# Attention scores of a two-layer kernel on two 64-row halves of TensorE

## The chip, the core and the metric

The kernel runs on one core of one Trainium2 chip. A core has five engines that run side by side and wait for each other by semaphores: TensorE (PE in the rows; its weight loads are PEld), VectorE (DVE), ScalarE (ACT), GpSimd (POOL) and SyncE (SP), which here only starts DMAs. The metric is the device time in microseconds, before as the median of three runs; lower is better.

## The reference, cut to what matters

There are 4096 tokens of 256 values (16 batches of 256). Each layer adds attention over a context and then a feed-forward part; only attention is touched here.

```
def _L0_xattn_ref(query, key, value, mask, Wq, bq, Wk, bk, Wv, bv, Wo, bo):
    ...
    q = proj_split(query, Wq, bq)
    k = proj_split(key, Wk, bk)
    v = proj_split(value, Wv, bv)
    scores = jnp.einsum('bhqd,bhkd->bhqk', q, k) * scale
    scores = jnp.where(mask == 0, jnp.float32(-1000000000.0), scores)
    probs = jax.nn.softmax(scores, axis=-1)
    attn = jnp.einsum('bhqk,bhkd->bhqd', probs, v)
    ...
x = x + _L0_xattn_ref(_layernorm(x, axis=-1), ctx_1024, ctx_1024, mask_1x1xSxS2_if1, ...)
x = x + _L0_ffn_ref(_layernorm(x, axis=-1), ...)
x = x + _L1_xattn_ref(_layernorm(x, axis=-1), ctx_1024, ctx_1024, ...)
x = x + _L1_ffn_ref(_layernorm(x, axis=-1), ...)
```

There are 16 heads of 16 values. In layer 0 the 256 queries of a batch attend to its 256 keys. In layer 1 attention runs over the 16 batches at one position, so the 256 tokens of a unit are 16 positions by 16 batches, and only the 16 by 16 blocks on the diagonal count. Layer 0's feed-forward part routes each token to 4 of 16 experts.

## The kernel before, in words

One program runs four stages, one after another: `attention` for layer 0 (`l0`), `routed_experts`, `attention` for layer 1 (`l1`) and `gated_ffn`. The change lies in `attention` alone, which both layers call.

`attention` works through 16 units of 256 tokens in a software pipeline. An iteration `u` has 16 steps `k`, one for each head, and in it work for several units stands side by side: at step `k`, TensorE makes the transposed scores of head `k` of unit `u` (L841, keys on the output's partitions) and the plain scores of head `k` of unit `u+2` (L874, queries on the output's partitions). Both are two matmuls, one for each half of 128 rows of output. The plain scores serve for the row maximum alone (VectorE, L715). The maxima are transposed on TensorE (L892, step 1 of the next iteration), split in two float16 parts (L553 on ScalarE, L744 on VectorE) and stacked by DMA under the queries (L385), so that the transposed scores come out with the maximum already taken off. ScalarE takes their exponential (L493) into `pt`, and TensorE multiplies it with the values, four heads at a time (L809 in layer 0, L806 in layer 1). These value products have 32 output columns each and stand side by side on four column groups of the array (`tile_position=(0, 32 * j)`).

Every iteration also holds, between the steps: transposing the normalized x of unit `u+3` (L883, step 0), projecting it to queries (L791 called at steps 4 and 5, called wq below), projecting the context to keys (steps 8 and 9, wk) and to values (steps 12 and 13, wv), the output projection of unit `u-1` (steps 9 and 10, wo), two rounds of transposing outputs (L818, steps 3 and 14), and transposing them again (L911, step 6). Layer 0 has three more pieces for its router: ranks (L852, step 4), a transposition (L830, step 6) and logits (L861, step 12).

Queries and keys are kept as two float16 parts, high and low. The projections leave them in `nat`, ScalarE making the high part (L527) and VectorE the low part (L614). DMAs on SP's queue stack the parts of a head on partitions: `qs` holds them as high, low, high (L392, three DMAs of 32 partitions), `ks` as high, high, low (L398, six DMAs of 16 partitions). One matmul over 96 partitions then gives the three products of the parts. `qs` has two heads on 32 partitions, an even one and an odd one, and `ks` has a place of its own for each of the 16 heads, where the rows of the other head of the pair are zero. Behind the 96 rows come constant rows (`key_rows`, in layer 1 also `query_rows`, which take care of the diagonal blocks) and the rows of the maxima: a plain score uses 96 partitions in layer 0 and 104 in layer 1, a transposed one 100 and 108. Before the pipeline starts, a setup block zeroes `ks` (half on GpSimd, L253, half on VectorE, L268) and loads the constant rows; VectorE waits for them at L276.

`ps_t` and `ps_s` have two buffers each, so a transposed score waits until the exponential two heads back is done (`exp_done`), and a plain score for the maximum two heads back (`max_done`). At step 0 the plain score also waits for the stacked queries and keys (`qs_stacked`, `ks_stacked`), and the transposed one for the stacked maxima (`m_stacked`). Every engine works in the order in which its code is written.

## Time and profile before

| what | value |
|---|---|
| time before, median of 3 runs (lowest to highest) | 1584.51 us (1583.52 to 1587.66) |
| the profiled execution's own time | 1574.22 us |
| its span, first to last instruction | 1572.3 us |
| mean granted TensorE clock in the span | 0.916 of full |
| TensorE matmuls busy | 1146.1 us (73%) |
| TensorE weight loads busy | 863.9 us (55%) |
| VectorE busy | 934.9 us (59%) |
| GpSimd busy | 814.4 us (52%) |
| ScalarE busy | 742.8 us (47%) |
| transposed scores of layer 0, first to last | 85.0 to 464.8 us |
| transposed scores of layer 1, first to last | 1091.1 to 1376.7 us |

The profile shows one execution, which was 10 us shorter than the median. Busy times are sums over the four stages, and the attention of layer 0 and of layer 1 takes some 430 us and 390 us of the span, setup and start included. A matmul's busy time holds its way through the array, so the distance between two starts tells more than its length: matmuls of 256 float16 columns start 0.11 us apart and last 0.27 us.

### The profile page before, as it was taken

What the parts mean: (1) busy time and instruction counts of PE and PEld (TensorE: products, weight loads), DVE (VectorE), ACT (ScalarE), POOL (GpSimd) and SP (SyncE); (2) the same over time, 40 slices, a digit from 0 to 9 for tenths busy, and PEclk for the clock granted to TensorE, in tenths of its full rate; (3) what the DMA queues carried; (4) which work ended last, traced back from release to release, by engine and by line L of the source; (5) the groups of instructions that cost most, each with busy time, mean ns of one, the idle gap of its engine ahead of it and who ended that gap; (6) DMA issues with size and microseconds to landing.
All of it is one profiled execution on the core that took longest, in us unless ns stands there. A gap on an engine that the chain in (4) does not pass through costs nothing. (4 is left out here: it accounts for less than half of the span.)

```text
span 1572.3 us, 35113 instructions
## 1 busy us (share of the span) xinstructions
PE 1146.1 (73%) x11011; PEld 863.9 (55%) x11012; DVE 934.9 (59%) x2206; ACT 742.8 (47%) x1455; POOL 814.4 (52%) x984
## 2 busy tenths in 40 slices
PE   0678788888872276799999998026777777718997
PEld 0355566656541165688887886014566666514555
DVE  4677678778641275566666664137777776435663
ACT  2356566666570154455555554012555555534442
POOL 5222455566466365567776774377666561003442
PEclk9999899999995598999999999567999999969999
DMA  5433323232210447233333343434454442131321
GB/s 156 109 108 77 80 59 86 78 67 69 37 41 21 71 129 140 78 98 106 107 107 104 107 107 89 95 113 132 136 144 140 129 137 64 33 101 54 101 86 55
DMA packets 146544, 147.39 MB, mean 94 GB/s; under 512 B 47912, under 2 KB 122200, under 8 KB 146392
## 3 DMA queue, kind: packets, MB, share of 16 engines
q1 hardware_dynamic: 119792, 95.31, 21.6%
q0 software_dynamic: 17920, 37.84, 9.7%
q10 hardware_dynamic: 8704, 12.58, 2.7%
q8 instruction: 73, 1.20, 0.4%
q14 instruction: 55, 0.45, 0.1%
HBM read 81.69 MB, written 38.27 MB: 76 GB/s over the span
## 5 line engine op out<-in xcount | busy, mean ns | idle before, releaser
L493 ACT ACTIVATE l_pt<-l_ps_t 128x512 f32<-128x512 f32 (+1 forms) x512 | 243.9, 495 | 247.6 <-PE l_ps_t L841 242.1
L715 DVE TENSOR_REDUCE l_mx<-l_ps_s 128x2 f32<-128x512 f32 (+1 forms) x512 | 274.3, 546 | 138.6 <-PE l_ps_s L874 132.7
L1298 PE MATMUL cp_ps_g<-cp_xt,ro_wexp 128*128 128x256 f16 x1920 | 226.7, 275 | 24.4 <-ACT cp_xt L1244 10.3
L1164 POOL DMA_INDIRECT cp_rows<-moe_rows,cp_now x160 | 172.8, 1080 | 95.5 <-POOL cp_now L1159 64.5
L1298 PEld LDWEIGHTS cp_ps_g<-cp_xt,ro_wexp 128*128 x1920 | 183.1, 99 | 55.9 <-issue 32.1
L1216 DVE TENSOR_SCALAR cp_gate<-cp_ps_g,ex_g_bias 128x256 f32<-128x256 f32 x160 | 70.0, 479 | 153.9 <-PE cp_ps_g L1298 153.9
L461 POOL DMA_INDIRECT l_picked<-expert_rows,l_slots x128 | 130.0, 1016 | 56.5 <-issue 36.4
L428 POOL DMA_INDIRECT row_tokens<-l_token_id,ro_pos x128 | 125.9, 984 | 49.2 <-issue 36.7
L1169 POOL TENSOR_TENSOR cp_a_lo<-cp_act_f,cp_a_hi 128x512 f16<-128x512 f32 x80 | 95.5, 1194 | 60.9 <-ACT cp_a_hi L1253 60.1
L874 PE MATMUL l_ps_s<-ro_wexp 96*128 96x256 f16 x512 | 101.6, 282 | 30.6 <-issue 14.6
L1313 PE MATMUL cp_ps_y<-ro_wexp,cp_a_hi 128*128 x640 | 114.9, 274 | 0.0
L1253 ACT CAST cp_a_hi<-cp_act_f 128x512 f16<-128x512 f32 x80 | 49.4, 618 | 128.9 <-DVE cp_act_f L1225 128.9
L841 PE MATMUL l_ps_t<-ro_wexp 100*128 100x256 f16 x512 | 100.7, 280 | 4.7 <-issue 3.3
L1487 POOL TENSOR_TENSOR ff_hlo<-ff_hf,ff_hhi 128x512 f16<-128x512 f32 x48 | 55.9, 1171 | 82.3 <-ACT ff_hhi L1516 82.3
L475 POOL TENSOR_TENSOR l_xin<-l_xin,l_bo 128x512 f32<-128x512 f32 x32 | 40.6, 1268 | 110.0 <-ACT l_xn L571 110.0
L1244 ACT COPY cp_xt<-cp_ps_x 128x1024 f16<-128x1024 f16 x80 | 80.2, 1004 | 34.5 <-PE cp_ps_x L1283 33.8
L874 PE MATMUL l_ps_s<-l_ks,l_qs 104*128 104x128 f16 x512 | 71.5, 229 | 33.4 <-issue 19.9
L1313 PE MATMUL cp_ps_y<-ro_wexp,cp_a_lo 128*128 x320 | 87.2, 273 | 0.0
L1249 ACT ACTIVATE cp_sg<-cp_gate 128x512 f32<-128x512 f32 x80 | 50.4, 630 | 73.9 <-DVE cp_gate L1216 73.9
L1283 PE MATMUL cp_ps_x<-ex_ident,cp_rows 128*128 128x128 f16 x640 | 50.0, 223 | 43.2 <-DMA cp_rows<-moe_rows,cp_now 43.0
L791 PE MATMUL l_ps_b<-l_chi,l_wk 128*128 128x256 f16 x256 | 55.3, 284 | 24.2 <-DVE l_nat L614 23.2
L874 PEld LDWEIGHTS l_ps_s<-ro_wexp 96*128 96x128 f16 x512 | 46.8, 100 | 46.7 <-issue 22.4
(246 smaller groups left out, 2845.0 us busy)
## 6 DMA issues: line engine op xcount, KB each, us to landing
expert_rows<-cp_yout SPq DMA_DIRECT2D x80, 256.0 KB
l_cin<-in_ctxT SPq DMA_DIRECT2D x32, 256.0 KB
ro_raw<-in_gate_up ACTq DMA_DIRECT2D x16, 512.0 KB, 4.0
x<-l_yout SPq DMA_DIRECT2D x64, 128.0 KB
ro_wexp<-l_nat SPq DMA_DIRECT2D x48, 128.0 KB
ro_wexp<-l_nat SPq DMA_DIRECT2D x96, 64.0 KB
l_qs<-l_nat SPq DMA_DIRECT2D x48, 128.0 KB
l_ks<-l_nat SPq DMA_DIRECT2D x96, 64.0 KB
```

The source lines that it names most:

```text
L428: nc.gpsimd.indirect_dma_start(route.table, bass.IndirectOffsetOnAxis(ap=route.pos[:, t, k:k + 1], axis=0), token_id[:, t:t + 1], None).th ...
L461: nc.gpsimd.indirect_dma_start(picked[:, n % 2, q, k], None, y_rows, bass.IndirectOffsetOnAxis(ap=slots[:, n * QT + q, k:k + 1], axis=0)). ...
L493: nc.scalar.activation(pt[:, h % 8], ps_t[:, at % 2, :, 0:span], ACT.Exp).then_inc(exp_done, 1)
L715: nc.vector.reduce_max(mx[:, n % 2, :, 8 * (k % 2) + k // 2], ps_s[:, at % 2, :, 0:span], AX_X).then_inc(max_done, 1)
L841: last = nc.tensor.matmul(ps_t[:, at % 2, kt, 0:span], ks[0:rows_t, u % KQ, key_head, kt * P:kt * P + P], qs[0:rows_t, u % KQ, h // 2, see ...
L874: last = nc.tensor.matmul(ps_s[:, at % 2, q, 0:span], qs[0:rows_s, n % KQ, h // 2, q * P:q * P + P], ks[0:rows_s, n % KQ, key_head, seen], ...
L1164: nc.gpsimd.indirect_dma_start(rows[:, n, h], None, route.rows_dram[:, :], bass.IndirectOffsetOnAxis(ap=now[:, n, h:h + 1], axis=0)).then_ ...
L1169: nc.gpsimd.tensor_tensor(a_lo[:, b], act_f[:, b], a_hi[:, b], ALU.subtract).then_inc(alo_done, 1)
L1216: nc.vector.tensor_scalar(gate[:, b, m], ps_g[:, b, m], g_bias[:, bass.ds(e, 1), m], LIMIT * WS, ALU.add, ALU.min).then_inc(gate_done, 1)
L1244: nc.scalar.copy(xt[:, 1 - b], ps_x[:, 1 - b]).then_inc(xt_copied, 1)
L1298: last = nc.tensor.matmul(ps_g[:, b, m], route.wexp[:, bass.ds(e, 1), cols:cols + P].rearrange("p o n -> p (o n)"), xt[:, b, part, c], sta ...
L1313: last = nc.tensor.matmul(ps_y[:, b, h], a[:, b, c, h * P:h * P + P], route.wexp[:, bass.ds(e, 1), cols:cols + D].rearrange("p o n -> p (o ...
```

## The change

The two heads of a pair get partitions of their own: the even head of each pair lies on partitions 0 to 63 and the odd one on 64 to 127, in `qs` and in `ks`. Each half holds 48 rows of parts, in layer 1 then 8 constant rows, and then the rows of the maxima, one of each part. `ks` needs 8 places in place of 16, and nothing has to be zero, so the zeroing (L253 and L268) and its semaphore go.

A score matmul now covers 64 rows of the array (`tile_position=(0, 0)` or `(64, 0)`). At step `k` the transposed scores are those of head `k` and the plain scores those of head `k ^ 1`, which lies on the other half. Their four matmuls stand in turns: transposed, plain, transposed, plain. All waits of both now stand ahead of the first of them. In layer 0 the ranks (step 4) and logits (step 12), which stood between a step's transposed and plain scores, now stand ahead of both.

The DMAs follow: six of 16 partitions for the queries in place of three of 32, four for the maxima in place of two, and the constant rows go to both halves (two DMAs in layer 0 in place of one, four in layer 1 in place of two), in rows of half the length.

```diff
-        rows_s = 96 + (8 if kinds else 0)
-        rows_t = rows_s + 4
+        data = 3 * DH
+        rows_s = data + (8 if kinds else 0)
+        rows_t = rows_s + 2
...
-                sp.wait_ge(ks_set, 2)
-                sp.dma_start(ks[96:rows_t].rearrange("p b h t -> p (b h t)"), key_rows).then_inc(rows_loaded, 16)
-                if kinds:
-                    sp.dma_start(qs[96:rows_s].rearrange("p b h t -> p (b h t)"), query_rows).then_inc(rows_loaded, 16)
+                for base in (0, 64):
+                    sp.dma_start(ks[base + data:base + rows_t].rearrange("p b h t -> p (b h t)"), key_rows).then_inc(rows_loaded, 16)
+                    if kinds:
+                        sp.dma_start(qs[base + data:base + rows_s].rearrange("p b h t -> p (b h t)"), query_rows).then_inc(rows_loaded, 16)
...
-                nc.gpsimd.memset(ks[:, 2:4], 0.0).then_inc(ks_set, 1)
...
-                nc.vector.memset(ks[:, 0:2], 0.0).then_inc(ks_set, 1)
...
-                            row = rows_s + 2 * i
-                            sp.dma_start(qs[row:row + 2, n % KQ], mt[:, i, :]).then_inc(m_stacked, 16)
+                            for par in range(2):
+                                row = 64 * par + rows_s + i
+                                sp.dma_start(qs[row:row + 1, n % KQ], mt[8 * par:8 * par + 8, i, :]).then_inc(m_stacked, 16)
...
-                            sp.dma_start(qs[32 * i:32 * i + 32, n % KQ].rearrange("d (j m) t -> d j (m t)", m=2),
-                                         nat[:, i % 2].rearrange("p m t -> p (m t)")).then_inc(qs_stacked, 16)
+                            for par in range(2):
+                                row = 64 * par + DH * i
+                                sp.dma_start(qs[row:row + DH, n % KQ].rearrange("d (j m) t -> d j (m t)", m=2),
+                                             nat[64 * par:64 * par + 64, i % 2].rearrange("p m t -> p (m t)")).then_inc(qs_stacked, 16)
...
                         n = u + 2
+                        if live(u):
+                            to = t_at[u, h]
+                            if h == 0:
+                                pe.wait_ge(m_stacked, 64 * (u + 1))
+                            pe.wait_ge(exp_done, c1 + to - 1)
                         if live(n):
-                            at = s_at[n, h]
+                            so = s_at[n, h ^ 1]
                             if h == 0:
-                                pe.wait_ge(qs_stacked, 48 * (n + 1))
+                                pe.wait_ge(qs_stacked, 96 * (n + 1))
                                 pe.wait_ge(ks_stacked, 96 * (n + 1))
-                            pe.wait_ge(max_done, c1 + at - 1)
...
+                            pe.wait_ge(max_done, c1 + so - 1)
...
+                        for half in range(QT):
+                            part = slice(half * P, half * P + P)
+                            seen = part if kinds else slice(0, UNIT)
+                            if live(u):
+                                base = 64 * (h % 2)
+                                last = nc.tensor.matmul(ps_t[:, to % 2, half, 0:span], ks[base:base + rows_t, u % KQ, h // 2, part],
+                                                        qs[base:base + rows_t, u % KQ, h // 2, seen], start=not masks, stop=True, tile_position=(base, 0))
+                                if half:
+                                    last.then_inc(st_done, 1)
+                            if live(n):
+                                base = 64 * (1 - h % 2)
+                                last = nc.tensor.matmul(ps_s[:, so % 2, half, 0:span], qs[base:base + rows_s, n % KQ, h // 2, part],
+                                                        ks[base:base + rows_s, n % KQ, h // 2, seen], start=not masks, stop=True, tile_position=(base, 0))
+                                if half:
+                                    last.then_inc(s_done, 1)
```

Three places show the new order. After the change the transposed scores are L876, the plain ones L882, the projections L793, the transposition of x L892 and the logits L850. The first is TensorE in layer 0, steps 11 and 12 of an iteration in the middle: the scores of step 11 and of step 12 (`ro_wexp` is the memory in which layer 0 keeps `qs` and `ks`), the logits (`l_rw`), and ahead and behind the end of wo and the start of wv. Before:

```order
L791 MATMUL l_ps_a<-l_wo,l_alo 128x256
L841 MATMUL l_ps_t<-ro_wexp 128x256 [waits at_exp_done]
L841 MATMUL l_ps_t<-ro_wexp 128x256
L874 MATMUL l_ps_s<-ro_wexp 128x256 [waits at_max_done]
L874 MATMUL l_ps_s<-ro_wexp 128x256
L841 MATMUL l_ps_t<-ro_wexp 128x256 [waits at_exp_done]
L841 MATMUL l_ps_t<-ro_wexp 128x256
L861 MATMUL l_ps_s<-l_rw,l_xt 128x16 [waits at_exp_done,at_max_done]
L861 MATMUL l_ps_s<-l_rw,l_xt 128x16 x3
L874 MATMUL l_ps_s<-ro_wexp 128x256 [waits at_max_done]
L874 MATMUL l_ps_s<-ro_wexp 128x256
L791 MATMUL l_ps_b<-l_wv,l_chi 128x256 [waits at_kl_done]
```

After:

```order
L793 MATMUL l_ps_a<-l_wo,l_alo 128x256
L876 MATMUL l_ps_t<-ro_wexp 128x256 [waits at_max_done,at_exp_done]
L882 MATMUL l_ps_s<-ro_wexp 128x256
L876 MATMUL l_ps_t<-ro_wexp 128x256
L882 MATMUL l_ps_s<-ro_wexp 128x256
L850 MATMUL l_ps_s<-l_rw,l_xt 128x16 [waits at_exp_done,at_max_done]
L850 MATMUL l_ps_s<-l_rw,l_xt 128x16 x3
L876 MATMUL l_ps_t<-ro_wexp 128x256 [waits at_max_done,at_exp_done]
L882 MATMUL l_ps_s<-ro_wexp 128x256
L876 MATMUL l_ps_t<-ro_wexp 128x256
L882 MATMUL l_ps_s<-ro_wexp 128x256
L793 MATMUL l_ps_b<-l_wv,l_chi 128x256 [waits at_kl_done]
```

The four score matmuls of a step now stand in turns behind one set of waits, and the logits, which parted step 12's four, stand ahead of them. What stands ahead of and behind such a group is, as before, work on all 128 rows.

The second is TensorE at the seam of two iterations, step 15 of one and step 0 of the next, in layer 0. Before:

```order
L841 MATMUL l_ps_t<-ro_wexp 128x256 [waits at_exp_done]
L841 MATMUL l_ps_t<-ro_wexp 128x256
L874 MATMUL l_ps_s<-ro_wexp 128x256 [waits at_max_done]
L874 MATMUL l_ps_s<-ro_wexp 128x256
L841 MATMUL l_ps_t<-ro_wexp 128x256 [waits at_exp_done,at_m_stacked]
L841 MATMUL l_ps_t<-ro_wexp 128x256
L874 MATMUL l_ps_s<-ro_wexp 128x256 [waits at_max_done,at_ks_stacked,at_qs_stacked]
L874 MATMUL l_ps_s<-ro_wexp 128x256
L883 MATMUL l_ps_b<-l_ident,l_xn 128x128 [waits at_v1_done,at_xn_done]
```

After:

```order
L876 MATMUL l_ps_t<-ro_wexp 128x256 [waits at_max_done,at_exp_done]
L882 MATMUL l_ps_s<-ro_wexp 128x256
L876 MATMUL l_ps_t<-ro_wexp 128x256
L882 MATMUL l_ps_s<-ro_wexp 128x256
L876 MATMUL l_ps_t<-ro_wexp 128x256 [waits at_ks_stacked,at_qs_stacked,at_max_done,at_exp_done,at_m_stacked]
L882 MATMUL l_ps_s<-ro_wexp 128x256
L876 MATMUL l_ps_t<-ro_wexp 128x256
L882 MATMUL l_ps_s<-ro_wexp 128x256
L892 MATMUL l_ps_b<-l_ident,l_xn 128x128 [waits at_v1_done,at_xn_done]
```

The wait for the stacked keys and queries of the unit two ahead moves up: it now holds the transposed scores of step 0 as well.

The third is SP's queue in one iteration, the DMAs of the maxima (`l_mt`) and of the queries. Before:

```order
L385 DMA ro_wexp<-l_mt 2x8x256 [waits at_mh_done]
L385 DMA ro_wexp<-l_mt 2x8x256 [waits at_ml_done]
L392 DMA ro_wexp<-l_nat 32x4x512 [waits at_qh_done,at_st_done]
L392 DMA ro_wexp<-l_nat 32x4x512 [waits at_qh_done]
L392 DMA ro_wexp<-l_nat 32x4x512 [waits at_ql_done]
L398 DMA ro_wexp<-l_nat 16x4x512 [waits at_kh_done]
```

After:

```order
L384 DMA ro_wexp<-l_mt 1x8x256 [waits at_mh_done]
L384 DMA ro_wexp<-l_mt 1x8x256
L384 DMA ro_wexp<-l_mt 1x8x256 [waits at_ml_done]
L384 DMA ro_wexp<-l_mt 1x8x256
L393 DMA ro_wexp<-l_nat 16x4x512 [waits at_qh_done,at_st_done]
L393 DMA ro_wexp<-l_nat 16x4x512
L393 DMA ro_wexp<-l_nat 16x4x512 [waits at_qh_done]
L393 DMA ro_wexp<-l_nat 16x4x512
L393 DMA ro_wexp<-l_nat 16x4x512 [waits at_ql_done]
L393 DMA ro_wexp<-l_nat 16x4x512
```

Five DMAs more stand ahead of the keys' six, which stay as they were.

## Rows read from the trace of the kernel before

**Rows 1.** The page's busy times of each engine over the span.

```profile
PE 1146.1 (73%) x11011; PEld 863.9 (55%) x11012; DVE 934.9 (59%) x2206; ACT 742.8 (47%) x1455; POOL 814.4 (52%) x984
```

**Rows 2.** Windows, the two steady stretches: length, engines' busy us, PEclk, DMA share, GB/s.

```profile
85.00:465.00 380.00, 318.68 (x3117) 226.24 (x3115) 269.25 (x702) 241.28 (x483) 188.89 (x257) 0.97 0.28 69
...
1091.00:1376.70 285.70, 216.97 (x2887) 173.54 (x2886) 200.38 (x541) 158.61 (x422) 141.86 (x173) 0.98 0.39 112
```

**Rows 3.** Timeline, PE in layer 0: start, length, line, tile, count [idle before].

```profile
250.76 0.27 PE L791 MATMUL l_ps_b<-l_xhi,l_wq 128*128 128x256 f16 x1
250.96 1.07 PE L809 MATMUL l_ps_o<-l_pt,l_v 128*32 128x256 f32 x16
251.96 0.66 PE L830 MATMUL l_ps_t<-l_ident,l_xn 128*128 128x128 f32 x4
...
253.34 0.38 PE L841 MATMUL l_ps_t<-ro_wexp 100*128 100x256 f16 x2
...
253.79 0.39 PE L841 MATMUL l_ps_t<-ro_wexp 100*128 100x256 f16 x2
```

**Rows 4.** Timeline, PE, the same value products cut after the first eight.

```profile
250.96 0.64 PE L809 MATMUL l_ps_o<-l_pt,l_v 128*32 128x256 f32 x8
```

**Rows 5.** Timeline, PE in layer 0, every idle time over 0.1 us of one iteration.

```profile
255.52 0.27 PE L791 MATMUL l_ps_b<-l_chi,l_wk 128*128 128x256 f16 x1 [1.11 <-DVE l_nat L614]
...
262.34 0.39 PE L874 MATMUL l_ps_s<-ro_wexp 96*128 96x256 f16 x2 [0.59 <-DVE l_mx L715]
...
267.36 0.38 PE L874 MATMUL l_ps_s<-ro_wexp 96*128 96x256 f16 x2 [0.22 <-issue]
...
271.65 0.63 PE L818 MATMUL l_ps_a<-l_ident,l_osb 128*128 128x128 f32 x4 [0.83 <-ACT l_osb L534]
...
279.10 0.27 PE L791 MATMUL l_ps_b<-l_chi,l_wk 128*128 128x256 f16 x1 [1.11 <-DVE l_nat L614]
```

**Rows 6.** Timeline, ACT in layer 0, the exponentials of steps 10 and 2.

```profile
259.45 0.60 ACT L493 ACTIVATE l_pt<-l_ps_t 128x512 f32<-128x512 f32 x1 [2.26 <-PE l_ps_t L841]
...
270.19 0.60 ACT L493 ACTIVATE l_pt<-l_ps_t 128x512 f32<-128x512 f32 x1 [0.69 <-PE l_ps_t L841]
```

**Rows 7.** Timeline, SP's queue: keys in layer 0, keys and queries in layer 1.

```profile
260.81 3.77 SPq L398 DMA_DIRECT2D ro_wexp<-l_nat  x6
...
1202.10 3.77 SPq L398 DMA_DIRECT2D l_ks<-l_nat  x6
...
1215.40 2.17 SPq L392 DMA_DIRECT2D l_qs<-l_nat  x3
```

**Rows 8.** Timeline, PE in layer 1: wv, value products, the seam, the next wv.

```profile
1203.04 0.39 PE L791 MATMUL l_ps_b<-l_wv,l_chi 128*128 128x256 f16 x2 [0.89 <-DVE l_nat L614]
...
1203.70 0.28 PE L841 MATMUL l_ps_t<-l_qs,l_ks 108*128 108x128 f16 x2
1203.82 0.28 PE L874 MATMUL l_ps_s<-l_ks,l_qs 104*128 104x128 f16 x2
1204.03 0.64 PE L806 MATMUL l_ps_o<-l_pt,l_v 128*32 128x128 f32 x16
...
1207.71 0.27 PE L874 MATMUL l_ps_s<-l_ks,l_qs 104*128 104x128 f16 x2 [1.27 <-issue]
...
1221.97 0.39 PE L791 MATMUL l_ps_b<-l_wv,l_chi 128*128 128x256 f16 x2 [0.89 <-DVE l_nat L614]
```

**Rows 9.** Timeline, ACT and DVE in layer 1 behind the seam.

```profile
1208.61 0.38 ACT L493 ACTIVATE l_pt<-l_ps_t 128x256 f32<-128x256 f32 x1 [1.61 <-PE l_ps_t L841]
...
1209.51 0.69 DVE L738 TENSOR_TENSOR l_xlo<-l_ps_b,l_xhi 128x512 f16<-128x512 f32 x1 [0.35 <-ACT l_xhi L548]
```

**Rows 10.** Layer 1's setup: timeline of SP and DVE, and a window (DMA share last but one).

```profile
1006.34 0.29 SPq L231 DMA_DIRECT2D l_qs<-in_query_rows  x1
...
1015.04 0.17 DVE L277 TENSOR_SCALAR l_bq<-l_bq 128x2 f32<-128x2 f32 x1 [16.34 <-DMA l_qs<-in_query_rows]
...
1009.40:1011.60 2.20, 0.00 (x0) 0.00 (x0) 0.00 (x0) 0.00 (x0) 0.00 (x0) 0.50 0.50 60
```

64 lines of the change are left out of this document (25 added, 39 removed).

## The prediction

> **What bounds the kernel now.** I read the page's busy times first: TensorE is the busiest engine [rows 1], but that is a mean over four stages. The windows then take the two stretches that the change touches: TensorE is busy in 318.68 of 380 us in layer 0 and in 216.97 of 285.7 us in layer 1, at nearly the full clock (0.97 and 0.98, where 1 is 2.4 GHz) [rows 2]. The timeline of one iteration says what sets its length. In layer 0 it takes 279.10 − 255.52 = 23.58 us, and TensorE is idle in four places only, 2.75 us in all [rows 5]. Each is the end of a chain through another engine: 1.11 us for the queries' low part (VectorE), 0.59 us for a maximum, 0.22 us at the seam, 0.83 us for ScalarE's copy of the outputs. In layer 1 the iteration takes 1221.97 − 1203.04 = 18.93 us [rows 8].
>
> The seam matters most. The keys' six DMAs start at 260.81 and take SP 3.77 us to issue; they land before the scores of step 0, at 267.36 [rows 5, 7]. In layer 1 it is 1202.10 to 1207.71, and TensorE stands idle for 1.27 us [rows 7, 8]. "issue" as releaser there is this wait: it is the one place in the order where the stacked keys are waited for. So from step 10 (keys projected) to step 0 the length is set by DMAs, 6.6 and 5.6 us, and TensorE's work of steps 11 to 15 hides under it. On the path lie the other pieces: seam to step 2 (its exponential, then the copies of ScalarE, then L818), steps 3 to 5 (wq), and steps 8 to 10 (wk, then the exponential of step 10, behind which ScalarE's key copy stands).
>
> **What a group of scores saves.** In layer 0 four score matmuls start in 253.79 − 253.34 = 0.45 us, 0.11 each [rows 3]. If the halves of the array run side by side, the four need two rounds, 0.22 us: saved 0.22. In layer 1 (128 columns) two start in 1203.82 − 1203.70 = 0.12 us [rows 8]; four in 0.23, afterwards 0.12: saved 0.11. Does it overlap? The nearest rows are the value products, four to a round on column groups: eight end at 251.60, sixteen at 252.03, so two rounds take 0.43 and one 0.215 [rows 3, 4]. A product has 256 columns, as a score has, so sixteen one behind the other at 0.11 would take at least 1.76 us; they take 1.00, so the four of a round do run together. I take full overlap for row halves, too; the other end is none.
>
> **What a group costs.** The same rows show the price of leaving the undivided array. Going in: 250.96 − 250.76 = 0.20, where 0.11 is usual, so 0.09. The 16 products take 251.96 − 250.96 = 1.00, four rounds 0.86, so 0.14 more for the first weights and for coming out [rows 3, 4]. Together 0.23; layer 1 gives 1204.03 − 1203.82 − 0.11 = 0.10 going in [rows 8]. With 0.01 for the second matmul behind, I take 0.24 for a round trip, 0.12 a change. Before, scores (96 to 108 rows) and projections (128 rows) change over at the usual distance, cost 0; that is the lower end for row halves. I take 0.12, since the value products are the only divided matmuls here.
>
> The Trainium skill bears on just this. "TensorEngine Tiling (Array Packing)", section Tiling Modes, says that changing the mode, not just the tile, drains the engine; for column groups the trace agrees, at 0.12 a change, and no run so far shows row halves. The same page's Overview gives up to 2x for contractions of at most 64 rows and prices no change of mode; by that alone the sum below would be the free case among the rivals.
>
> **How many changes.** In layer 0 an iteration of before has 8 changes, two at each of four groups of value products. After it has 31: the scores of steps 2 and 3, 7 and 8, and 15 and 0 stand together, each other group stands alone, and at steps 1, 9 and 13 the value products follow it directly, which spares one. 23 x 0.12 = 2.8 us against 16 x 0.22 = 3.5 us saved: by throughput a gain of 0.7 us. Layer 1 (no logits, ranks or router transposition) has 28: 20 x 0.12 = 2.4 against 16 x 0.11 = 1.8, a loss of 0.6 us. What counts is what lies on the path.
>
> **Layer 0, on the path.** At the seam the transposed scores of step 0, before already done, now come with the plain ones: two rounds where two matmuls were, nothing saved. Coming out +0.12, into step 1's group +0.12, the group −0.22, straight into the value products 0, into step 2's group +0.12: the exponential of step 2, which waited 0.69 us for TensorE [rows 6], starts 0.14 later, and L818 with it. Steps 4 and 5: 2 x (0.24 − 0.22) = +0.04. Steps 9 and 10: +0.12 − 0.22 + 0.12 = +0.02 until the exponential of step 10, which waited 2.26 us for TensorE [rows 6]. Steps 6 to 8 hide under the 1.11 us wait. Steps 10 to 15 get 0.2 us shorter and hide under the DMAs. Sum +0.20 us an iteration.
>
> **Layer 1, on the path.** Behind the seam step 1's exponential waited 1.61 us for TensorE, and VectorE was idle 0.35 us behind it; from there VectorE is busy without a break to step 6 [rows 9]. Out and in, +0.24. Steps 9 and 10: 0.12 − 0.11 + 0.12 = +0.13. Steps 11 to 15 add 0.8 us and hide in the 1.27 us. Sum +0.37.
>
> Over 16 iterations a layer, those at the ends taken alike: 3.2 + 5.9 = **+9.1 us**.
>
> **The rest.** The transposed scores now stand behind the maximum's wait, and ScalarE behind them. At step 12 that is 0.59 us [rows 5]; their exponential comes later, but nothing on the path waits for step 12's (the value products of step 13 take heads 8 to 11), so I take 0; it is up to 0.6 an iteration if ScalarE's slack there went. SP issues 5 DMAs more ahead of the keys, 0.63 us each [rows 7]: the queries' now take 3.77 in place of 2.17 us, from 1215.40 to 1219.2, and the keys' start at about 1221: hidden by 1.8 us. In the start of layer 1 the queries' issue just met the keys', +0.4 once. Zeroing `ks` hid behind loads: 0. The constant rows are waited for: in layer 1 VectorE starts at 1015.04, 8.7 us behind the last issue [rows 10]. The window 1009.4 to 1011.6 has a DMA share of 0.50, eight of 16 engines with one query row of 16 KB each, for 2.2 us, behind the key rows of 32 KB: every such DMA starts at the same engines. Eight engines had 48 KB each and get 64 KB: +2 us (0 to 3). In layer 0, 4 rows of 32 KB become 4 of 16: 0, at best −1.5. Together **+2.4 us** and, with the ends' small change, I take +2.
>
> The sum is +11 us against the profiled execution's own 1574.22, 1585. That execution was 10 us below the median; on the median of 1584.51 the same difference gives 1595.5.
>
> **Rivals.** *Free changes* (row halves cost nothing to enter or leave; the undisturbed change-overs of 96 to 128 rows speak for it, the value products against). Then layer 0 saves 0.22 at steps 1, 4, 5 and 9, −0.88, and layer 1 0.11 at step 9, over 14 full iterations −13.9, plus 2.4: −11, 1573. *Cheaper changes*, 0.08: layer 0 has nine on its path, 0.72 − 0.88 = −0.16, layer 1 four, 0.32 − 0.11 = +0.21: with 2.4 a sum of +3, 1588, no difference. The point at which the steady part turns is (0.88 + 0.11) / 13 = 0.076 us a change. *No overlap*: then layer 0 loses 0.20 + 0.88, and steps 10 to 15 add 1.08 us where 0.22 + 0.59 cover it, so 1.3 to 1.9 an iteration; layer 1 0.48: +29 to +40, 1618. *A lower clock*: shorter bursts with drains between might lose some of the granted 0.97; if layer 1 went to 0.9, TensorE's 14 us of an iteration grow by 8%, half of it on the path, +0.55 x 16 = +9 more, 1605.
>
> **How the numbers follow.** The likeliest (0.12 a change, full overlap) has 0.50, its own range 1588 to 1603 (rows 0 to +3, path terms ±30%). Free changes 0.15, cheaper 0.16, no overlap 0.10, lower clock 0.09. Leaving out half of the free case and most of no overlap gives 1573 to 1612. A measurement tells 0.3% (4.8 us) from no change. Faster: the free case and an edge, 0.17. Same: the cheaper case and the likeliest one's low edge, 0.22. Slower: 0.61.
>
> **What the profile will show.** If right: the starts of transposed and plain scores of one step under 0.02 us apart, the next round 0.11 later; about 0.2 us in place of 0.11 from a projection to a score and back; an iteration of 23.8 us in layer 0 and 19.3 in layer 1; the seam's idle time in layer 1 down to about 0.5 us. Wrong if a score follows a projection after 0.11 us (free), if the four scores of a step start 0.11 apart (no overlap), or if PEclk in the windows falls.

## The result, and the profile of the changed kernel

The changed kernel takes 1633.96 us (median of four runs, 1616.3 to 1636.8), the kernel before 1584.07: a ratio of 1.0288, 95% interval 1.0225 to 1.0351. Later, beside others on one chip, it was 1.027 (1.0224 to 1.0316). The forecast was 1595.5 us in a range of 1573 to 1612. It is outside: the sign was right, the size was four times too small, about 46 us by the ratio (50 by the two medians) against 11.

The profiled execution took 1616.3 us, with a span of 1614.3. First the row that answers to [rows 1] and the granted clock over the span, then the two windows that answer to [rows 2] and two shorter ones at the start of each layer's pipeline (length, busy us, then PEclk, DMA share, GB/s at the end), and last these two shorter ones in the kernel before.

```profile
PE 1175.1 (73%) x11011; PEld 775.0 (48%) x11012; DVE 932.8 (58%) x2204; ACT 745.8 (46%) x1455; POOL 803.3 (50%) x982
...
PEclk9678899999995598999999998556999989868999
```

```profile
60.00:101.00 41.00, 32.45 (x156) 13.31 (x154) 29.65 (x55) 13.65 (x26) 8.71 (x14) 0.54 0.37 103
85.00:465.00 380.00, 302.87 (x3029) 162.92 (x3028) 269.83 (x687) 235.68 (x470) 184.35 (x252) 0.93 0.25 68
1084.00:1129.00 45.00, 33.98 (x248) 17.56 (x248) 27.63 (x75) 16.36 (x39) 30.79 (x37) 0.58 0.41 122
...
1091.00:1376.70 285.70, 215.13 (x2517) 131.07 (x2516) 198.25 (x531) 140.45 (x366) 155.49 (x185) 0.87 0.38 114
```

```profile
60.00:101.00 41.00, 29.47 (x234) 19.48 (x233) 35.34 (x68) 17.94 (x35) 9.94 (x18) 0.95 0.48 127
...
1084.00:1129.00 45.00, 32.93 (x385) 25.41 (x386) 32.08 (x89) 22.68 (x57) 30.98 (x40) 0.92 0.48 136
```

PEclk fell from 0.97 to 0.93 in layer 0 and from 0.98 to 0.87 in layer 1, and the starts of both layers, at 0.95 and 0.92 before, ran at 0.54 and 0.58. This is what the prediction had listed last among the signs of being wrong. Matmuls of 256 columns start 0.11 us apart at 2.4 GHz and 0.21 at 1.2 GHz (two projections at 1127.38 and 1127.59, where PEclk is 0.50), so on the path a half-clock stretch doubles TensorE's part.

The windows are the same microseconds of both traces and not the same work. Layer 1's transposed scores ran from 1091.3 to 1376.7 us before and from 1109.0 to 1420.7 after; over these stretches of their own PEclk is 0.98 and 0.89, in layer 0 0.97 and 0.94. The trace of before is also that of an execution 10 us below its median.

Most local signs came as forecast. The timeline of TensorE in layer 0 shows one group between two projections, and answers to [rows 3].

```profile
262.14 0.27 PE L793 MATMUL l_ps_b<-l_xhi,l_wq 128*128 128x256 f16 x1
262.34 0.28 PE L876 MATMUL l_ps_t<-ro_wexp 50*128 50x256 f16 x1
262.35 0.28 PE L882 MATMUL l_ps_s<-ro_wexp 48*128 48x256 f16 x1
262.46 0.27 PE L876 MATMUL l_ps_t<-ro_wexp 50*128 50x256 f16 x1
262.47 0.27 PE L882 MATMUL l_ps_s<-ro_wexp 48*128 48x256 f16 x1
262.67 0.28 PE L793 MATMUL l_ps_b<-l_xhi,l_wq 128*128 128x256 f16 x1
```

Transposed and plain scores start within 0.01 us of each other, the next pair 0.12 later, and the ways in and out take 0.20 each where 0.11 is usual. Overlap is full, and a change of mode costs 0.09 to 0.10. An iteration, counted between the starts of x's transpositions, takes 19.34 to 19.38 us in layer 1 when its whole length is at full clock (one of four took 20.33); 19.3 was forecast. In layer 0, where 23.8 was forecast, the six at full clock take 23.2 to 26.5.

One sign failed. TensorE's idle time at the seam of layer 1 was to fall from 1.27 to about 0.5 us. Where the clock is full it is mostly 1.37 to 1.40:

```profile
1213.77 0.21 PE L876 MATMUL l_ps_t<-l_qs,l_ks 58*128 58x128 f16 x1 [1.40 <-DMA l_ks<-l_nat]
```

The transposed scores of step 0, 0.11 us of work, now stand behind this wait. From `wv`, at 1208.96, to the end of the wait it is 4.81 us, so TensorE worked for 3.41 of them; before, it was 3.40 of 4.67 with those scores in it [rows 8]. So the changes of steps 13 to 15 add 0.1 us; for steps 11 to 15, 0.8 were taken to hide here. Even so, most of this looked like a right path and a wrong clock. The experiments say otherwise.

### The profile page after: what moved, and what is told of

Its sections match the earlier page's. It is cut to its first block and busy times, and to the rows that moved or that the text cites. A ratio compares the mean times of both kernels' runs of the same rounds, so it can differ in the third digit from the quotient of the medians.

```text
span 1614.3 us, 35690 instructions
## 1 busy us (share of the span) xinstructions
PE 1175.1 (73%) x11011; PEld 775.0 (48%) x11012; DVE 932.8 (58%) x2204; ACT 745.8 (46%) x1455; POOL 803.3 (50%) x982
## 3 DMA queue, kind: packets, MB, share of 16 engines
q1 hardware_dynamic: 122256, 95.32, 20.4%
## 5 line engine op out<-in xcount | busy, mean ns | idle before, releaser
L1307 PE MATMUL cp_ps_g<-cp_xt,ro_wexp 128*128 128x256 f16 x1920 | 232.7, 280 | 20.7 <-DVE ro_wexp L1241 6.7
L876 PE MATMUL l_ps_t<-ro_wexp 50*128 50x256 f16 x512 | 97.9, 283 | 28.2 <-DVE l_mx L717 15.7
L882 PE MATMUL l_ps_s<-ro_wexp 48*128 48x256 f16 x512 | 103.7, 300 | 10.7 <-DVE l_mx L717 6.5
L876 PE MATMUL l_ps_t<-l_qs,l_ks 58*128 58x128 f16 x512 | 66.9, 234 | 30.2 <-DMA l_ks<-l_nat 23.8
L793 PE MATMUL l_ps_b<-l_chi,l_wk 128*128 128x256 f16 x256 | 58.8, 296 | 33.0 <-DVE l_nat L615 32.2
L882 PE MATMUL l_ps_s<-l_ks,l_qs 56*128 56x128 f16 x512 | 70.0, 243 | 7.6 <-DVE l_mx L717 4.2
```

The source lines that it names most:

```text
L876: last = nc.tensor.matmul(ps_t[:, to % 2, half, 0:span], ks[base:base + rows_t, u % KQ, h // 2, part], qs[base:base + rows_t, u % KQ, h // ...
L882: last = nc.tensor.matmul(ps_s[:, so % 2, half, 0:span], qs[base:base + rows_s, n % KQ, h // 2, part], ks[base:base + rows_s, n % KQ, h // ...
L1307: last = nc.tensor.matmul(ps_g[:, b, m], route.wexp[:, bass.ds(e, 1), cols:cols + P].rearrange("p o n -> p (o n)"), xt[:, b, part, c], sta ...
```

## The experiments

Times are ratios to the kernel before, whose runs stood beside each (medians 1593.7 to 1598.0 us). There are four columns on the granted clock and the path:

- "Windows" is PEclk in the windows 85:465 and 1091:1376.7, layer 0 and layer 1.
- "Own stretch" is PEclk from the first to the last transposed score of each layer. It is the better measure where a kernel's layer 1 starts late: the window then holds much of its slow start.
- "Span" is the clock over the whole span, lowest and highest of all the kernel's runs; for the kernel before beside them it is 0.895 to 0.915.
- "Iteration" is the length at full clock: the median in layer 0, the recurring shortest value in layer 1. Layer 0's rests on two to six iterations that lie up to 4 us apart, so small differences mean little there.

The kernel before has no trace at its later, longer time; the kernel with split transfers only stands in for it.

| kernel | ratio (95%) | windows L0 / L1 | own stretch L0 / L1 | span | iteration L0 / L1, us |
|---|---|---|---|---|---|
| split transfers only | 1.0013 (0.999 to 1.0036) | 0.94 / 0.94 | 0.95 / 0.97 | 0.896 to 0.909 | 23.6 / 18.9 |
| new order, whole transfers | 1.0135 (1.0091 to 1.0178) | 0.95 / 0.92 | 0.95 / 0.94 | 0.893 to 0.900 | 24.1 / 19.3 |
| new order and splits, full arrays | 1.016 (1.0109 to 1.0211) | 0.95 / 0.94 | 0.95 / 0.97 | 0.891 to 0.904 | 24.5 / 19.3 |
| the same, halves in layer 0 | 1.0153 (1.0117 to 1.019) | 0.91 / 0.92 | 0.91 / 0.95 | 0.881 to 0.889 | 24.8 / 19.3 |
| the same, halves in layer 1 | 1.0329 (1.027 to 1.0389) | 0.94 / 0.78 | 0.95 / 0.83 | 0.862 to 0.879 | 24.2 / 19.4 |
| changed kernel | 1.027 (1.0224 to 1.0316) | 0.90 / 0.83 | 0.90 / 0.88 | 0.865 to 0.873 | 24.9 / 19.4 |

### Full arrays in the new order

What could be put down to the halves had to be told from what came with them. This kernel keeps the layout of before and takes everything else of the change (the code is shortened to the branch for full arrays).

```
-                                base = 64 * (h % 2)
-                                ... ks[base:base + rows_t, u % KQ, h // 2, part] ... tile_position=(base, 0))
+                                base, kh = 0, 8 * (h % 2) + h // 2
+                                ... ks[base:base + rows_t, u % KQ, kh, part] ...)
```

> The changed kernel's order on TensorE (the waits of both heads first, then T, S, T, S by halves; the scores of head k^1), its splits of the q, k and m transfers, but the layout and the full-array score matmuls of the kernel before, in both layers. Theory (the 64-row halves cause both the longer iterations and the lower clock): iterations of 23.6 us in layer 0 and 18.9 in layer 1, granted clock 0.97 and 0.98 in the windows 85:465 and 1091:1376.7, time 1584 to 1590 us. Rival (the new order or the split transfers cause it): 1605 us or more, with the clock of those windows below 0.95.

Measured: 1.016. The rival was right for over half of the loss: 26 us (0.016 x 1598) are lost without one matmul on halves. Its clock (0.95 and 0.94 in the windows, 0.95 and 0.97 over its own stretches) is that of the kernel with split transfers only, so that part of the rival doesn't clearly show. Layer 1's iteration is 19.25 to 19.27 us. So of the +0.42 us on which prediction and trace seemed to agree, +0.33 is the order.

### Which part of the order

Two kernels divide it: the split transfers on the kernel before, and the order without them.

```
-                            sp.dma_start(qs[32 * i:32 * i + 32, n % KQ]..., nat[:, i % 2]...)
+                            for par in range(2):
+                                row = 32 * i + DH * par
+                                sp.dma_start(qs[row:row + DH, n % KQ]..., nat[64 * par:64 * par + 64, i % 2]...)
```

> The kernel before, with one part of the change alone: the transfers of q and m split as the change splits them (q by parity, six of 16 rows in place of three of 32; m four of one row in place of two of two). Theory S (the splits fill SP's queue and the DMA queues ahead of the keys, on which the seam waits): most of what the new order with full arrays costs (ratio 1.016) comes with this part, 1.008 or more, and from the keys' low part to the next iteration it takes 0.3 us longer. Theory O (it is the order on TensorE, where the transposed scores and ScalarE behind them stand behind the maximum's and the keys' waits): within 0.3% of the kernel before.

> The other part alone: layout and full-array matmuls of the kernel before and its whole q and m transfers, but the changed kernel's order and waits on TensorE. Theory O: ratio 1.012 to 1.018, almost all of what the new order with full arrays and split transfers costs. Theory S: within 0.5% of the kernel before.

Measured: 1.0013 and 1.0135. Splitting costs nothing that can be told, as forecast; the order is the cost. Two places show it. First the start of a layer 1 iteration in the kernel with split transfers only (SP's issue of the keys, TensorE, ScalarE), then the same place in the new order with whole transfers.

```profile
1186.37 3.73 SPq L401 DMA_DIRECT2D l_ks<-l_nat  x6
...
1191.96 0.27 PE L877 MATMUL l_ps_s<-l_ks,l_qs 104*128 104x128 f16 x2 [1.25 <-issue]
1192.08 0.63 PE L886 MATMUL l_ps_b<-l_ident,l_xn 128*128 128x128 f32 x4
...
1192.86 0.38 ACT L496 ACTIVATE l_pt<-l_ps_t 128x256 f32<-128x256 f32 x1 [1.59 <-PE l_ps_t L844]
```

```profile
1192.60 3.77 SPq L407 DMA_DIRECT2D l_ks<-l_nat  x6
...
1198.36 0.22 PE L884 MATMUL l_ps_t<-l_qs,l_ks 108*128 108x128 f16 x1 [1.52 <-DMA l_ks<-l_nat]
...
1198.59 0.60 PE L900 MATMUL l_ps_b<-l_ident,l_xn 128*128 128x128 f32 x4
...
1199.41 0.38 ACT L502 ACTIVATE l_pt<-l_ps_t 128x256 f32<-128x256 f32 x1 [0.29 <-PE l_ps_t L884]
```

The issues end at 1190.10 and 1196.37. From there to the exponential of step 1 it was 2.76 us and is 3.04. 0.11 of the difference are two more matmuls ahead of x's transpositions; 0.13 lie between the issues' end and the first matmul (1.86, now 1.99), and why is open. In layer 0 the exponential of step 0, 0.6 us on ScalarE, comes behind the landing, too, ahead of that of step 1 and of the copy of x.

The second place is the one that the prediction set at 0: the transposed scores behind the maximum. The first row below is step 12 of layer 0 (TensorE's timeline), the others are totals of TensorE's waits over the program (us, times, longest), all of the new order with whole transfers.

```profile
274.77 0.27 PE L884 MATMUL l_ps_t<-ro_wexp 100*128 100x256 f16 x1 [1.00 <-DVE l_mx L725]
```

```profile
PE l_ps_t L884 <- DVE l_mx L725: 14.6, 20, 1.0
PE l_ps_s L890 <- DVE l_mx L725: 9.8, 18, 1.6
```

In the kernel before, no transposed scores waited for a maximum (theirs is the wait for an exponential); now they do 20 times, and ScalarE behind them. Each place was then put back alone, in the order with whole transfers.

```
+                        if live(u) and not masks and APART(h):
+                            for half in range(QT):
+                                transposed(half)
                         if live(n):
                             so = s_at[n, h ^ 1]
```

APART(h) is h == 0 in the first, h > 0 in the second.

> The kernel with the changed order, full-array matmuls and whole transfers (ratio 1.0135), with one place put back: at step 0 the transposed scores go ahead of the wait for the stacked keys, as in the kernel before. Theory P (the cost of the new order lies at the seam: two more matmuls between the keys' landing and the transpositions of x, and the exponential of step 0 behind the keys instead of ahead of them): layer 0's stretch from the transpositions to the low part of x returns from 2.3 to 2.0 us and that from the keys' low part to the next iteration by 0.2 us in both layers; 10 to 14 us less, ratio 1.004 to 1.007. Theory Q (it lies at the other 15 steps, where the transposed scores stand behind the maximum two scores back): ratio 1.010 or more.

> The other half: the transposed scores go ahead of the maximum's wait at steps 1 to 15, as in the kernel before, but stay behind the keys' wait at step 0. Theory P: ratio 1.008 to 1.012. Theory Q: 1.004 or less.

Measured: 1.0068 (1.0038 to 1.0098) and 1.0036 (1.0004 to 1.0069). Both theories hold in part. In layer 1 the iterations are exact: 18.93 with neither, 19.07 with the merged waits of steps 1 to 15, 19.16 to 19.20 with the merged one of step 0, 19.29 with both: 0.14 and 0.23 against 0.36. By the ratios the steps weigh more (0.010 against 0.007), which lies within the intervals.

How the 22 us of the order (0.0135 x 1595) divide is not settled by this. At full clock its iterations account for 16 x 0.36 = 6 us in layer 1. In the single traces, layer 0 takes no longer from first to last transposed score than with split transfers only (392.0 us against 393.6), for all its higher median, and layer 1 takes 11 us longer (300.1 against 289.2), at a clock of 0.94 against 0.97. Some of the order's cost may thus be clock, too.

For the halves the first place was put back, too.

> The changed kernel (64-row halves, split transfers) with the same place put back: step 0's transposed scores alone, then the keys' wait, then step 0's scores alone; at this step nothing overlaps and no change of array mode is added, since both are on halves. Theory P: 8 to 14 us less than the changed kernel, ratio about 1.020; its granted clock stays low, 0.83 to 0.88 in layer 1, since the order has no part in it. Theory Q: within 4 us of the changed kernel.

Measured: 1.0283 (1.0222 to 1.0344), no gain, and theory P missed here. Only four iterations of layer 1 were at full clock; one of them took 19.19 us where 19.36 is usual, the others 20.3 to 20.4. PEclk stood at 0.89 and 0.83, low as forecast. Why the repair isn't seen at a low clock was not tested.

### The rest of the loss: which layer

> The changed kernel's layout, halves and order in layer 1 alone; layer 0 has the layout and the full-array matmuls of the kernel before in the new order. If the loss of each layer is its own: layer 0 as before (first T of layer 1 near 1091 us), layer 1 with iterations of 19.4 us at full clock and stretches at half clock, granted clock 0.87 there, about 28 us longer than before from first to last T (285.6 us before, 311.7 in the changed kernel): 1608 to 1615 us in all. If layer 0's loss carries over into layer 1's clock: layer 1 is at 0.95 or more, and the time about 1593 us.

> The changed kernel in layer 0, full arrays in the new order with split transfers in layer 1: the counterpart of the halves in layer 1 alone, whose ratio was 1.033. Relative to full arrays in both (1.016), halves in layer 1 cost 27 us; halves in both came to 1.027 to 1.029, so that by subtraction halves in layer 0 give back some 8 us: ratio 1.009 to 1.013, with layer 1's clock at 0.92 to 0.94. If each layer's loss were alike: 1.022.

> The changed kernel itself, beside the next three on one chip, since the first four experiments ran on a chip where the kernel before took 1598 us and not 1584. Its ratio to the kernel before should again be 1.025 to 1.033, and its steady iterations 23.9 us in layer 0 and 19.4 in layer 1 where the clock is full.

In layer 1 the halves cost 1.7% (27 us) over full arrays in the same order, in layer 0 nothing that can be told (the 8 us that were to come back there did not). It may be that what the overlap saves on a path that TensorE sets, the lower clock takes; layer 0's iterations at full clock don't show the saving. The three windows of layer 1, halves in layer 1 alone, in both, in layer 0 alone:

```profile
1091.00:1376.70 285.70, 221.17 (x2332) 130.13 (x2328) 195.56 (x523) 130.70 (x339) 166.20 (x196) 0.78 0.38 117
```

```profile
1091.00:1376.70 285.70, 215.36 (x2394) 129.04 (x2394) 198.08 (x535) 135.57 (x349) 169.60 (x204) 0.83 0.40 121
```

```profile
1091.00:1376.70 285.70, 210.20 (x2522) 166.20 (x2520) 202.63 (x551) 141.12 (x366) 166.09 (x199) 0.92 0.41 120
```

From the first to the last transposed score of layer 1 the three took 323.8, 313.3 and 298.4 us, with PEclk at 0.83, 0.88 and 0.95. The iterations at full clock differ by 0.1 us, 2 us over 16; most of the rest goes with the clock. The second prediction of l1_halves, that layer 0's loss carries over, fell. Its first was right on layer 1 (29 us longer than with full arrays in the same order) and missed the time, since it counted nothing for the order. The parts don't add up exactly (1.032 by addition, 1.027 measured); the intervals allow it.

### By what the clock falls

Three things changed at once: halved rows, changes of mode, overlap. The first kernel has the changes and the rows, without overlap:

```
-                            so = s_at[n, h ^ 1]
+                            so = s_at[n, h]
...
-                                base = 64 * (1 - h % 2)
+                                base = 64 * (h % 2)
```

> The changed kernel, except that the scores of a step are of the same head as the transposed ones (k in place of k^1), so that both lie on the same 64 rows and can't run side by side: all changes of array mode stay, the overlap goes. By the prediction's prices each group costs 0.22 us more in layer 0 and 0.11 in layer 1: iterations of about 27.3 us in layer 0, where TensorE sets the pace, and 19.5 to 21 in layer 1. Theory A (the clock fell because the overlap packs the same columns into less time and the stops at the changes leave TensorE idle, so that it is less busy): with the overlap gone the columns fill more time, and the granted clock of layer 0's and layer 1's steady stretches lies between the changed kernel's (0.93, 0.87) and before's (0.97, 0.98); time about 1650 to 1670 us. Theory B (half-array matmuls as such count for less, whether side by side or not): the clock is as low as the changed kernel's or lower; time over 1680 us.

Measured: 1.0587 (1.0534 to 1.064), clock 0.83 and 0.79. Its layer 1 starts at 1177 us, so the second window holds 85 us of what comes ahead; over its own stretches the clock is 0.84 and 0.84, and 0.841 to 0.865 over the span. Now the columns fill more of the time, and the clock is lower still in layer 0 (the changed kernel has 0.90) and no higher in layer 1 (0.88, and 0.83 with halves there alone). Theory A fell, theory B stands.

The next kernel adds changes of mode and nothing else; what its expectation calls theory C is set out with the one behind it (half_rows): the clock falls by the overlap and by the stops at changes.

> The kernel before plus one tiny matmul (128x32 weights, 8 columns) on column group 1 ahead of each step's transposed scores, which forces the array out of and into the undivided mode once more a step; its result is overwritten. All the full work stays. By the prices of the prediction (0.24 us a round trip) five such trips lie on layer 0's path and three on layer 1's: iterations at full clock +0.9 to +1.2 and +0.5 to +0.7 us, 23 to 30 us in all at an unchanged clock, ratio 1.014 to 1.019. If the stops also lower the clock (Theory C needs this): layer 1's window below 0.90 and a ratio of 1.025 or more.

```
+                            if not masks:
+                                nc.tensor.matmul(ps_t[32:64, at % 2, 0, 0:8], wq[:, 0, 0, 0:32], wq[:, 0, 0, 0:8], start=True, stop=True, tile_position=(0, 32))
```

Measured: 1.0294 (1.0252 to 1.0337). TensorE in layer 0, a projection, the tiny matmul, the scores; then both windows:

```profile
330.88 0.27 PE L791 MATMUL l_ps_b<-l_chi,l_wk 128*128 128x256 f16 x1
331.08 0.18 PE L838 MATMUL l_ps_t<-l_wq 128*32 128x8 f16 x1
331.19 0.39 PE L843 MATMUL l_ps_t<-ro_wexp 100*128 100x256 f16 x2
```

```profile
85.00:465.00 380.00, 341.30 (x3036) 217.22 (x3035) 259.18 (x642) 220.16 (x435) 168.68 (x232) 0.94 0.27 66
1091.00:1376.70 285.70, 235.62 (x2596) 164.71 (x2595) 203.66 (x544) 138.46 (x348) 175.24 (x212) 0.92 0.43 126
```

The scores start 0.31 us behind the projection where 0.11 is usual: a trip costs 0.20. The clock, 0.94 and 0.92 in the windows, 0.95 and 0.98 over the own stretches and 0.898 to 0.907 over the span, is that of the full-array kernels in the table. So these changes of mode, to a column group and back, cost their own time and nothing of the clock that can be told, and theory C loses what it needs. They cost more than expected, though (1.014 to 1.019): iterations of 25.33 and 19.95 us are +1.76 and +1.02, by 0.20 a trip nearly nine and five of the sixteen on the path, where the prediction's way of following it gave five and three. 16 x 1.76 and 16 x 1.02 us make 44 of the 47 measured (0.0294 x 1596).

> The kernel before, order, transfers and waits untouched, whose score matmuls contract only the first 48 rows in place of 96 to 108 (so the low parts of the keys, the maxima and layer 1's mask of other positions are left out of the scores), not placed on halves. It has neither side-by-side matmuls nor, if such a matmul counts as one of the undivided array, changes of array mode: starts stay 0.11 us apart. Theory R (the clock falls because a half-array matmul makes TensorE less active, whatever the rows beside it do): iterations at full clock as before (23.6, 18.9 us), but the granted clock of layer 1's window goes from 0.94 (the value on this chip in the kernel before with split transfers) to 0.90 or less, ratio 1.005 to 1.015. Theory C (only the time in which columns stream counts, so that the loss comes from overlap and from the stops at changes): clock and time as before, ratio 0.998 to 1.002.

```
-    ... ks[0:rows_t, u % KQ, key_head, kt * P:kt * P + P], qs[0:rows_t, u % KQ, h // 2, seen] ...
+    ... ks[0:48, u % KQ, key_head, kt * P:kt * P + P], qs[0:48, u % KQ, h // 2, seen] ...
```

> The kernel before, whose score matmuls contract 72 rows in place of 96 to 108 (part of the low terms, the maxima and layer 1's mask of other positions are left out of the scores). With more than 64 rows it should stay in the undivided array, starts 0.11 us apart before, between and behind the scores: no changes of mode, no overlap, the same columns. Theory R (the clock follows how many rows work, whatever the mode): granted clock of the windows down by about half of what 48 rows cost (0.94 to 0.83 and 0.81), to 0.87 to 0.91, iterations at full clock 23.6 and 18.9 us, ratio 1.008 to 1.017. Theory M (what lowers the clock is the use of 64-row halves, not the count of rows): clock and time as before, ratio 0.997 to 1.003.

With 48 rows: 1.053 (1.0481 to 1.0579), clock 0.83 and 0.81, over its own stretches 0.82 and 0.86 (layer 1 starts at 1174 us). But this kernel wasn't what it was meant to be: its iterations of layer 1 at full clock take 19.5 us and not 18.9. The timeline shows x's transpositions and the next scores, first with 48 rows, then with 72:

```profile
423.90 0.66 PE L883 MATMUL l_ps_b<-l_ident,l_xn 128*128 128x128 f32 x4
424.49 0.39 PE L841 MATMUL l_ps_t<-ro_wexp 48*128 48x256 f16 x2
```

```profile
336.33 0.60 PE L883 MATMUL l_ps_b<-l_ident,l_xn 128*128 128x128 f32 x4
336.76 0.38 PE L841 MATMUL l_ps_t<-ro_wexp 72*128 72x256 f16 x2
```

0.59 us with 48 rows, 0.43 with 72. From a projection to the scores behind it, it is 0.20 to 0.21 us with 48 rows, like the way into the halves of the changed kernel, and 0.11 with 72. So a 48-row matmul pays the change of mode without a word in the code, and half_rows had the changes, too. The 72-row kernel has none, its shortest iterations at full clock are those of before (23.2 and 18.9 us), and still it takes 1.0118 (1.0075 to 1.0161) with a lower clock:

```profile
85.00:465.00 380.00, 316.02 (x2947) 222.25 (x2946) 265.30 (x671) 227.34 (x456) 177.36 (x243) 0.93 0.29 67
1091.00:1376.70 285.70, 218.22 (x2516) 169.86 (x2514) 201.88 (x550) 139.31 (x366) 163.85 (x199) 0.89 0.41 120
```

Over its own stretches the clock is 0.92 and 0.92 (with split transfers only 0.95 and 0.97). Over the span it is 0.885 to 0.887 in all five runs, and 0.897 to 0.915 in the 14 of the kernel before beside them. Order, mode and number of matmuls are the same; the rows that contract, 72 in place of 96 to 108, differ, and with them the values, since part of the low terms, the maxima and the mask are left out. So theory R holds as far as these runs can tell the two apart: the granted clock follows the rows, and 19 us (0.0118 x 1594) go with them. Whether the values have a part was not tested. The Trainium skill ("TensorE: Matmul & The Clock Gate", Part 1) says that the clock is set by how busy TensorE has been, and that instructions are not what is counted. The first fillers below agree with that: they compute nothing that is used, and took a window from 0.83 to 1.00. The other direction was tried with rows of zeros, 124 and 128 rows a score.

```
-        rows_s = 96 + (8 if kinds else 0)
-        rows_t = rows_s + 4
+        rows_s = 124
+        rows_t = 128
```

> The kernel before, whose score matmuls contract more rows without need: constant and maxima rows moved to 124 to 127, zeros between, so that plain scores contract 124 rows in place of 96 and 104 and transposed ones 128 in place of 100 and 108. Columns, order and waits are the same; one DMA and one fill more in the setup. Theory R: a granted clock 0.01 to 0.03 higher in the windows, the start of layer 1 nearer full clock, 3 to 10 us less: ratio 0.994 to 0.998. Theory M, or rows of zeros not counting: ratio 0.999 to 1.002.

Measured: 0.998 (0.9945 to 1.0015), clock 0.96 and 0.95, over the span 0.901 to 0.919 where the kernel before has 0.897 to 0.915. The direction is that of theory R, but the interval holds no change; this one stays undecided.

### Giving TensorE work to do

If the clock falls for want of activity, unused full-array matmuls should bring it back.

```
+                            for i in range(FILL(u, k, kinds) if not masks else 0):
+                                nc.tensor.matmul(ps_s[:, s_at[n, h ^ 1] % 2, 0], wq[:, 0, 0, 0:P], wq[:, 0, 0], start=True, stop=True)
```

> The changed kernel with more work for TensorE where it would wait: full-array matmuls of 128x256 with the q weights, into the bank that the scores of the step overwrite afterwards, ahead of the wait for the exponentials: 6 at k 0, 2 at each other k while u is below 0, 1 at each k in layer 1, none in layer 0 otherwise. They compute nothing that is used. Theory (the loss is the clock's, and the clock falls because TensorE is too little busy): layer 1's granted clock comes back to 0.95 or more from 0.87, iterations stay 19.4 to 20 us, the half-clock prologues go, and the time falls by 15 to 30 us to 1605 to 1620 although TensorE does more. Rival (the clock falls with the changes of array mode themselves): the clock stays below 0.9 in layer 1, and the time is 1634 us or longer.

> The changed kernel with unused full-array matmuls (128x256, into the bank of scores that is overwritten next) put only where TensorE waits in every iteration: in layer 1 six at the seam, six ahead of the outputs' transposition, eight ahead of the transposition at step 6, eight ahead of wk, six ahead of wv, and two a step in its start; in layer 0 two at the seam, four and eight. If the granted clock falls because TensorE is too little busy, layer 1 runs at 0.97 or more with iterations of 19.4 to 19.8 us, and the kernel takes 12 to 25 us less than the changed one; if the changes of array mode lower the clock, it is no faster than the changed one.

> The changed kernel with unused full-array matmuls where it waits for the stacked keys: ten in layer 1 and one in layer 0 at step 0, and two a step in the start of layer 1, the pattern that lowered the time of the kernel before by 0.4% without lengthening its iterations. If activity is what the clock follows: layer 1's granted clock from 0.83 back to 0.93 or more with iterations of 19.4 to 19.5 us, and 12 to 25 us less than the changed kernel, ratio 1.012 to 1.019, which is what the new order alone costs. If ten at one place don't reach: ratio 1.022 or more.

> The kernel before with unused full-array matmuls (128x256) where it waits for the stacked keys, six in layer 1 and one in layer 0 at step 0, and two a step in the start of layer 1. If the clock follows TensorE's activity for the kernel before, too, the start of layer 1 (granted clock 0.50 to 0.80 in its first four iterations) runs nearer to full clock and takes 3 to 6 us less, and the half-clock stretches of layer 1's steady part go (another 2 to 6 us): ratio 0.994 to 0.998. If the fillers only lengthen the path: 1.000 to 1.003.

The windows of layer 1 with the first pattern and with ten at step 0:

```profile
1091.00:1376.70 285.70, 242.29 (x2845) 150.55 (x2843) 206.00 (x553) 143.45 (x363) 169.56 (x202) 1.00 0.41 121
```

```profile
1091.00:1376.70 285.70, 229.91 (x2624) 142.25 (x2625) 199.42 (x541) 137.31 (x353) 171.47 (x203) 0.92 0.40 121
```

The first pattern (one a step, six at step 0) brought layer 1 to 1.00, with iterations of 20.1 to 20.8 us for 19.4: the clock's gain went into the fillers, and the time stayed, 1.0247 (1.0201 to 1.0293), where 15 to 30 us less were expected. The second, where TensorE waits, was a failure, 1.0419 (1.0389 to 1.0448): every iteration after layer 1's start ran at full clock but took 20.88 us or more, and layer 0's over 26. Its row at step 3 tells why.

```profile
1254.74 0.83 PE L823 MATMUL l_ps_s<-l_wq 128*128 128x256 f16 x6 [1.35 <-DVE l_mx L720]
```

The fillers themselves wait for a maximum 1.35 us. To be race-free they needed the other bank of scores, and VectorE frees it behind the very work for which TensorE stood idle; so they came when the wait was over. Only the wait for the keys is behind nothing that the fillers need. Ten there and two a step in layer 1's start gave 1.0197 (1.0146 to 1.0249), between the two cases expected, with 19.36 us and a clock of 0.92: against 1.027 some 12 us of the loss came back, though the two intervals just touch, and the iteration got no longer.

The same for the kernel before gives the only version that beats both: 0.9964 (0.9934 to 0.9994), 1590.37 us against 1595.33, inside the range expected. TensorE in layer 1, the six fillers and the wait's end behind them, and the window:

```profile
1206.73 0.82 PE L870 MATMUL l_ps_s<-l_wq 128*128 128x256 f16 x6
1208.19 0.27 PE L879 MATMUL l_ps_s<-l_ks,l_qs 104*128 104x128 f16 x2 [0.64 <-issue]
```

```profile
1091.00:1376.70 285.70, 223.55 (x2883) 179.03 (x2884) 209.11 (x568) 151.21 (x399) 158.53 (x194) 0.99 0.41 121
```

All twelve iterations behind the start are at full clock, seven of them of 18.93 to 18.99 us; the kernel with split transfers had 9 of 12 at full clock. It is a small gain, at the edge of what can be told.

## Why the prediction was wrong, step by step

- **Overlap and price of a change**: the overlap was right, 0.22 us saved a group in layer 0. The price was somewhat high: 0.20 in and 0.20 out against 0.11 are 0.19 a round trip where 0.24 was taken, and in layer 1 it is 0.18 (0.20 in against 0.11, 0.15 out against 0.06). The sum for *no overlap* leaves out the +2.4 at its lower end: its own terms give +31, not +29.
- **The path**: in layer 1 right in its number by luck. +0.37 us an iteration was forecast as the sum of changes and overlap, +0.42 was measured, and full arrays in the same order have +0.33 of it; the halves added 0.1, not 0.37. In layer 0 +0.20 was forecast; the medians at full clock are 0.7 (first trace) to 1.3 us above before's, with 0.9 for full arrays in the same order, all with a scatter as large. The tiny matmuls show that more changes lie on the path than the prediction counted, so the overlap must have given back more than it counted, too. A likely reason, not tested: in the turns T, S, T, S with full arrays each second half starts one matmul later, which the overlap undoes.
- **The new order**: the first step that failed. "I take 0; it is up to 0.6 an iteration if ScalarE's slack there went" is the mis-sized term, and with it the seam, where the transposed scores of step 0 were priced at "two rounds where two matmuls were, nothing saved", and their later exponential at nothing. Both together cost 1.35 to 1.6%, 22 to 26 us; the prediction had only changes of mode there. Its own upper end, 0.6 us in 32 iterations, would have given 19.
- **Transfers**: right, 1.0013. The constant rows of layer 1 were taken at +2 us: from their first issue to VectorE's start it is 10.6 and 10.7 us in the two traces of the changed kernel, 9.1 before and 8.9 with split transfers only, so +1.5 to 1.8.
- **The clock**: the second step that failed. The rival was named and had 0.09, at +9 us for layer 1 at 0.9 with bursts and drains as its reason. Over its own stretch layer 1 went to 0.88 beside 0.97 with split transfers only, layer 0 to 0.90 beside 0.95, and both starts to half clock in the first trace. The changed kernel lost about 18 us over full arrays in the same order and with the same transfers (1.027 against 1.016), most of it in that way by the traces: layer 1's stretch took 313 us against 295, of which 16 x 0.1 us are the path's. The drains have no visible part in it (changes_only), and undoing the overlap gave no clock back (same_half); fewer rows lower the clock by themselves (rows_72). How much of the fall the rows explain in the changed kernel was not measured.

What stays open: how the order's cost divides between path and clock; whether the values in the rows count beside their number; why the keys' wait ends 0.13 to 0.15 us later when it releases transposed scores in place of plain ones; and how a row of zeros counts. On the last, half of the 96 rows of before are zero in `ks` alone, and the halves leave out mainly these; the rows that rows_128 adds are zero in `qs` and `ks`.

## What to carry to other kernels

Merging two waits so that two matmuls can start together makes each wait for the later of the two: here 1.35 to 1.6% of the time. Price that first, with full arrays in the new order, before pricing the overlap. Halving the rows of matmuls that leave TensorE with slack saved nothing on the path here (layer 1) and lost clock on everything else: look at PEclk in the stage, and count what the halves take away from the work on the array, not only what they save in time. A wait for a DMA can be filled with unused full matmuls if neither their target nor their operands wait for anything; elsewhere they lengthen the path.

## What the hardware showed that was not expected

- The granted clock falls with fewer contracting rows at the same columns, order and mode: with 72 rows for 96 to 108 it was 0.885 to 0.887 over the span where the kernel before had 0.897 to 0.915, and 0.92 over layer 1's own stretch where 0.97 was usual; with 48 rows, with changes of mode, 0.86 there. Added changes of mode alone left it at 0.98.
- Unused full-array matmuls of 0.11 us, one a step and six at step 0, took the window of layer 1 from 0.83 to 1.00.
- A matmul of 48 rows without a placement pays the change of mode (0.20 us from a projection to it, 0.11 with 72 rows).
- The round trip through column groups around one tiny matmul costs 0.20 us, the matmul included.
